# Three softmax attentions: each softmax step once for twelve heads in place of twice for six

## The reference

```python
attn = jax.nn.softmax(jnp.einsum('bhnd,bhmd->bhnm', q, k) * hd ** (-0.5), axis=-1)
o = jnp.einsum('bhnm,bhmd->bhnd', attn, v).transpose(0, 2, 1, 3).reshape(B, N, C)
return o @ proj_w + proj_b
```

## Time and profile before

| what | value |
|---|---|
| timed runs | 1854.51, 1858.04 and 1855.23 us, median 1855.23 |
| the profiled execution's own time | 1862.26 us |
| its span, first to last instruction | 1860.3 us |
| busy in the span | PE 88%, PEld 62%, DVE 55%, ACT 40%, POOL 30% |
| granted TensorE clock, mean over the span | 0.924 |

### The profile page before, as it was taken

One profiled execution on the slowest core, in us unless ns is written; L12 is line 12 of the kernel. 1 busy time (PEld: TensorE's weight loads), 2 busy tenths in 40 slices (PEclk: granted clock), 3 DMA queues, 4 the chain that ended last, 5 costly groups with the idle time before them and its releaser, 6 DMA issues. The chain is left out here.

```text
span 1860.3 us, 35935 instructions
## 1 busy us (share of the span) xinstructions
PE 1635.3 (88%) x13405; PEld 1149.9 (62%) x13425; DVE 1020.1 (55%) x2819; ACT 749.7 (40%) x1439; POOL 558.0 (30%) x530
## 2 busy tenths in 40 slices
PE   7999689997996899948888887899998998879997
PEld 5677579976774799736645544222224775548886
DVE  2477722225888222237625666788886675952221
ACT  1256223323442112125524544899994454211111
POOL 1131022226001342373000112655553100324553
PEclk9999779997997899978879888999999998989998
DMA  5000445521004455212010113999992003025662
GB/s 222 1 2 2 156 153 179 179 88 43 1 0 161 161 188 178 77 38 92 2 45 1 41 49 123 343 394 383 356 332 105 1 2 133 19 71 173 186 184 39
DMA packets 97446, 228.03 MB, mean 123 GB/s; under 512 B 24297, under 2 KB 55753, under 8 KB 96393
## 3 DMA queue, kind: packets, MB, share of 16 engines
q1 hardware_dynamic: 77527, 206.13, 31.4%
q0 software_dynamic: 19552, 19.63, 4.4%
q10 hardware_dynamic: 210, 0.15, 0.0%
HBM read 198.91 MB, written 26.56 MB: 121 GB/s over the span
## 5 line engine op out<-in xcount | busy, mean ns | idle before, releaser
L2822 ACT ACTIVATE l2s_hidden<-ps,pack_l2f 128x816 f32<-128x816 f32 x256 | 226.8, 937 | 18.1 <-PE ps L2746 8.6
L2841 POOL TENSOR_TENSOR l2s_gated<-l2s_hidden,l2s_whole 128x408 f32<-128x408 f32 x128 | 137.4, 1073 | 102.3 <-PE ps L2754 102.3
L2864 DVE TENSOR_TENSOR l2s_gated<-l2s_hidden,l2s_whole 128x816 f32<-128x816 f32 x128 | 143.1, 1118 | 27.3 <-ACT l2s_hidden L2822 25.4
L2362 PE MATMUL ps<-l_down,l_hidden 128*128 x792 | 139.8, 327 | 0.0
L2321 POOL DMA_INDIRECT l_xt<-rows_in,l_tokens x66 | 63.1, 955 | 255.8 <-PE ps L2334 197.7
L2362 PEld LDWEIGHTS ps<-l_down,l_hidden 128*128 128x128 f32 x792 | 127.3, 190 | 0.4
L131 PE MATMUL ps<-pack_const 128*128 128x512 bf16 x366 | 96.5, 421 | 22.5 <-PEq L165 6.0
L2345 PE MATMUL ps<-l_xtT,l_up 128*128 128x128 f32 x792 | 103.3, 282 | 3.4 <-DVE l_xtT L2597 3.4
L2345 PEld LDWEIGHTS ps<-l_xtT,l_up 128*128 128x128 f32 x792 | 100.2, 198 | 4.5 <-DVE l_xtT L2597 4.5
L2441 ACT ACTIVATE l_hidden<-ps,l_down 128x128 f32<-128x128 f32 x198 | 54.6, 374 | 91.8 <-PE ps L2350 91.8
L3176 POOL DMA_INDIRECT out<-l3c_part,l3c_chosen_place x32 | 57.1, 1785 | 98.5 <-DVE l3c_part L3295 89.9
(11 more groups left out here) (514 smaller groups left out, 3690.5 us busy)
## 6 DMA issues: line engine op xcount, KB each, us to landing
l2s_whole<-g_whole SPq DMA_DIRECT2D x128, 612.0 KB, 7.5
l_up<-in_l_up SPq DMA_DIRECT2D x66, 576.0 KB, 3.8
l3c_wg<-in_l_gate SPq DMA_DIRECT2D x16, 576.0 KB, 5.0
l3c_wu<-in_l_up SPq DMA_DIRECT2D x16, 576.0 KB, 6.6
l3c_wd<-in_l_down SPq DMA_DIRECT2D x16, 576.0 KB, 3.8
slots_out<-l_y SPq DMA_DIRECT2D x66, 96.0 KB, 2.3
l_down<-in_l_down SPq DMA_DIRECT2D x8, 675.0 KB, 8.6
l_down<-in_l_down SPq DMA_DIRECT2D x8, 576.0 KB, 7.9
```

The lines of the kernel that those rows point to most:

```text
L2362: last = pe.matmul(y_bank(i), hidden[:, i % 2, t, :], wd[:, t * D:(t + 1) * D], start=(t == 0), stop=(t == FM - 1))
L2822: act.activation(hidden[:, p % kept, :, :], ps[:, 0, 2 * (p % 2):2 * (p % 2) + 2, 0:NG], ACT.Gelu_apprx_tanh, bias=w.at("b1")[:, s * MT + ...
L2841: pool.tensor_tensor(gated[:, (4 * n + 1) % ring, :], hidden[:, 2 * n % kept, 1, :], whole[:, n % ahead, 0, :], ALU.mult).then_inc(late_re ...
L2864: dve.tensor_tensor(gated[:, at:at + 2, :], hidden[:, (2 * n + 1) % kept, :, :], whole[:, n % ahead, 1:3, :], ALU.mult).then_inc(gated_rea ...
```

## The change

The loop over two halves goes from five places: maximum and subtraction (VectorE), exponential and copy (ScalarE), and turning (TensorE). Each step is now one instruction, or one run of 12 turnings, with one wait and one signal; counts in the other waits follow, and L690, which waited for the first half of the copy, waits for all of it.

```diff
--- before.py
+++ after.py
@@ -553,10 +553,6 @@
 
             return ps[0:L, side, :, 0:HT * L].rearrange("p r (t n) -> p r t n", t=HT)
 
-        def groups(a):
-
-            return slice(2 * a, 2 * a + 2)
-
         def turned(n, c):
 
             return g["xT_all"][:, c, 2 * n:2 * n + 2, :] if keep else xT[:, n % 2, c, :, :]
@@ -657,17 +653,16 @@
             def turn(s):
 
                 side = s % 2
-                for a in range(2):
-                    pe.wait_ge(p_ready, 2 * s + a + 1)
-                    for r in range(RG)[groups(a)]:
-                        for t in range(HT):
-                            last = pe.transpose(ps[0:L, side, r, t * L:(t + 1) * L], p[:, side, r, t, :], ident[0:L, 0:L])
-                    last.then_inc(pT_ps, 1)
+                pe.wait_ge(p_ready, s + 1)
+                for r in range(RG):
+                    for t in range(HT):
+                        last = pe.transpose(ps[0:L, side, r, t * L:(t + 1) * L], p[:, side, r, t, :], ident[0:L, 0:L])
+                last.then_inc(pT_ps, 1)
 
             def outputs(s):
 
                 side = s % 2
-                pe.wait_ge(pT_ready, 2 * s + 2)
+                pe.wait_ge(pT_ready, s + 1)
                 for t in range(HT):
                     for r in range(RG):
                         last = pe.matmul(head_oT_at(side)[HP * r:HP * (r + 1), t, :], v[:, s // 2 % 2, side, HT * r + t, :],
@@ -685,7 +680,7 @@
 
                 pe.wait_ge(o_ready, s + 1)
                 if s + 1 < B:
-                    pe.wait_ge(pT_ready, 2 * (s + 1) + 1)
+                    pe.wait_ge(pT_ready, s + 2)
                 for c in range(C):
                     last = pe.transpose(oT_at(side)[:, c * L:(c + 1) * L], o[:, s % 2, c * K:(c + 1) * K], ident[0:L, 0:L])
                 last.then_inc(oT_ps, 1)
@@ -763,16 +758,12 @@
 
             def exponentials(s):
 
-                for a in range(2):
-                    act.wait_ge(below_ready, 2 * s + a + 1)
-                    act.activation(p[:, s % 2, groups(a), :, :], p[:, s % 2, groups(a), :, :], ACT.Exp, scale=HD ** -0.5)\
-                       .then_inc(p_ready, 1)
+                act.wait_ge(below_ready, s + 1)
+                act.activation(p[:, s % 2, :, :, :], p[:, s % 2, :, :, :], ACT.Exp, scale=HD ** -0.5).then_inc(p_ready, 1)
 
             def pT_copies(s):
-                for a in range(2):
-                    act.wait_ge(pT_ps, 2 * s + a + 1)
-                    act.activation(pT[:, s % 2, groups(a), :, :], banked(s % 2)[:, groups(a), :, :], ACT.Copy)\
-                       .then_inc(pT_ready, 1)
+                act.wait_ge(pT_ps, s + 1)
+                act.activation(pT[:, s % 2, :, :, :], banked(s % 2), ACT.Copy).then_inc(pT_ready, 1)
 
             def head_oT_copies(s):
                 act.wait_ge(head_oT_ps, s + 1)
@@ -935,14 +926,10 @@
                 side = s % 2
                 dve.wait_ge(s_ps, s + 1)
                 peaks = top[:, side, :].rearrange("p (r t) -> p r t", r=RG)
-                for a in range(2):
-                    dve.tensor_reduce(peaks[:, groups(a), :], banked(side)[:, groups(a), :, :], AX.X, ALU.max)\
-                       .then_inc(top_ready, 1)
-                for a in range(2):
-                    dve.wait_ge(top_ready, 2 * s + a + 1)
-                    dve.tensor_tensor(p[:, side, groups(a), :, :], banked(side)[:, groups(a), :, :],
-                                      peaks[:, groups(a), :].unsqueeze(3).broadcast_to([L, 2, HT, L]), ALU.subtract)\
-                       .then_inc(below_ready, 1)
+                dve.tensor_reduce(peaks, banked(side), AX.X, ALU.max).then_inc(top_ready, 1)
+                dve.wait_ge(top_ready, s + 1)
+                dve.tensor_tensor(p[:, side, :, :, :], banked(side), peaks.unsqueeze(3).broadcast_to([L, RG, HT, L]),
+                                  ALU.subtract).then_inc(below_ready, 1)
 
             def divide(s):
                 side = s % 2
```

## The result

The changed kernel takes 1904.05 us (median of 4 runs, 1900.60 to 1908.22), the kernel before 1854.87 in the same set: ratio 1.0269, 95% interval 1.0238 to 1.0300. It is 49 us slower; the forecast was 36.

A forecast was written before the change was run, and what follows sets the result against it. A chain of waits between engines, not a full VectorE or ScalarE, was taken to bound the softmax attentions. Waits of 31.9 us plus 3.8 of clock gave 35.7 on the median 1855.23: 1891 us, range 1880 to 1903.

The forecast's parts named there:

- Prices: Whole instructions of 1224 elements: exponential 1.22 us, copy 1.19, subtraction 1.42, reduction 1.43, from the time per element.
- L690: TensorE instruction overwriting bank 1 waits for the whole copy: 0.62 us later in l0f, 0.10 in l3a.
- even and odd iterations: Steady samples grow, even and odd: l0f 1.05 and 0.62 us, l3a 0.53 and 0.23, l2a 0.53 and 0.42.
- The sum of waits: Added waits over three attentions: l0f 13.7 us, l3a 9.1, l2a 9.1, together 31.9.
- the three ends: Each attention's last sample has no scores behind its turning to hide the copy: 1.83 us each.
- The clock: Granted clock falls in l0f's last sample and the end that follows, about 2 x 1.92 = 3.8 us.
- the upper case: l2a and l3a also fall to the lower clock a sample sooner: 3.8 us more, 39.5 in all.
- Grouping pays: Rival: late halves are off the path, fewer starts save 8 us over 48 samples: 1847; chance 0.04.
- Twice the single: Rival: merged instructions cost as much as two halves, some 18 us more in three attentions: 1909; chance 0.05.
- The clock falls in the middle: Rival: idle TensorE lowers the clock in some 10 of 33 mid-attention iterations, 19 us more: 1910; chance 0.06.
- The rule weighed in the prediction: Grouping can help saturated engines; where unsaturated Scalar and Vector cause bubbles elsewhere, breaking instructions up may finish work sooner.

The follow-up runs named there:

- the clock held: Changed kernel plus unread 512-column TensorE products, 6 before each of the last three turnings and 4 behind the last one, in every attention: 1879.35 us, ratio 1.0130.
- the products: Unread 512-column matmuls in TensorE's idle time of an attention's last samples; change in l3a alone with them there: 1862.97 us, against 1875.68 without.
- the products in l2a alone: Kernel before plus unread 512-column TensorE matmuls in l2a's last samples only: 1846.60 us, ratio 0.9948 to the kernel before.

## Why the prediction was wrong in size and right in its mechanism

**Prices, L690, even and odd iterations: right.** In l0f an even interval grew by 1.17 us (6.43 to 7.60; forecast 1.05), an odd one by 0.61 (0.62), a last one at full clock by 1.03 (1.02).

**The sum of waits: near, though an iteration is missing from it.** Forecast 31.9 us, measured with the clock held 33.9. The sum counts 14 iterations (one first, 5 even, 5 odd, 3 last), but 15 lie between the 16 turnings of an attention. The sixth odd one, s = 11, was left out, and it grew by 0.99 us in l0f (5.28 to 6.27), 1.13 in l2a and 0.99 in l3a: 3.1 together. Between the turnings 29.9 us were measured (l0f 13.6, l2a 7.7, l3a 8.6) where the sum has 26.4; behind them, with the three ends, 4.0 were measured where it has 5.5. The dearer ends of the sum hid part of the missing iteration: that the total came within 2 us was in part luck.

**The clock: the step that failed.** The sum had 3.8 us, "for its last sample and the end that follows" in l0f, and 0 to 3.8 more if l2a and l3a fell "a sample sooner". The direction was right, the size was 10 to 17. Three things were missing. The fall in l0f came two samples before the end. l2a fell a sample sooner and l3a fell at all, both together, where the forecast held it for the upper case. And nothing was counted behind the attentions, though the next layers begin at the lower level: in l3a's case 112.81 us without the products against 106.10 with them (109.07 in the profile of the kernel before, 105.4 in three others with l3a as before), which no row of the attention shows. The measured 33.9 of waits and 10 to 17 of clock make 44 to 51 in place of 35.7; 49 was measured.

**The rivals.** Grouping pays: refuted; no part alone gained. Twice the single: refuted by the prices above, though its 1909 is near the time measured. The clock falls in the middle: refuted, a pair of l0f stayed at 1.00, and the even and the odd intervals keep their lengths through all three attentions. The rule weighed in the prediction (the Trainium skill, Perfetto Trace Analysis, Optimizing Scalar/DVE Operations) holds in its second half: VectorE and ScalarE were not full (10.45 and 8.10 of 12.66 us), and the broken instructions let TensorE start sooner (an even interval of l0f took 6.43 us with them, 7.60 without).

**Open.** How far behind an attention the loss belongs to its end is not settled, least of all behind l2a. That stretch took 242.57 us in one profile of the changed kernel and 236.15 in another, but 232.30 with the change in l2a alone and, with turning and copy alone whole, 228.27 without any product; with l2a as before it took 233.75 to 235.67. The 10.2 us that the products in l2a alone give the kernel before lie mostly there (126.61 to 123.94 in the attention, 235.65 to 225.52 behind it), and why so far behind was only observed.

## What to carry to other kernels

Before merging instructions, look who waits for the first half: where the next engine idles, the merged instruction's whole duration goes onto the path in place of its first half's (1.22 us in place of 0.71 for the exponential), and what one start saves (0.02 to 0.09 us here) is far less. Merging a single link (the exponential, or turning and copy) cost 33 to 34 us where all together cost 49, since a whole instruction on either side ends the overlap. When you sum such waits, count the iterations against the profile. Where a change adds idle time on TensorE, look whether the granted clock falls there, and price the lower level for the rest of the stretch and for the layers behind it; a few products in the idle time lengthened no interval of l0f's last samples, and gave the kernel before 0.9% (1840.10 us, the fastest kernel here).

## What the runs showed of the hardware

One program's time follows its mean granted clock. 60 runs of the kernel before lie about a line of 1.40 us less for each 0.001 of clock (1868.24 us at 0.918, 1842.70 at 0.940), with a scatter of 2.5 us. Ten runs of the changed kernel have a mean clock of 0.917, those of the kernel before 0.926; by the line that is 13 us of the 49, an estimate that lies in the 10 to 17 above. With the products the kernel before had 0.940: some 20 us by the line, 16.4 measured.

The same instructions do not meet the fall at the same place each time. With l2a in halves and without products, its last two intervals took 6.19 and 7.67 us in the profile of the kernel before, 5.76 and 7.19 with the change in l3a alone, 7.22 and 7.25 with the change and products in l3a, and 5.75 and 5.75 with the change in l0f alone, where none was slow. One profile shows that the clock can fall in a stretch, and not how often it does.
